# A two-layer graph network on one core: its first pass over the adjacency matrix is rebuilt

## What is computed

```python
def layer0(x, adj, w):
    A = adj + eye(4096)
    d = rsqrt(sum(A, axis=1))
    return elu(((A * d[:, None] * d[None, :]) @ x) @ w)

def layer1(x, adj, W, b):
    return relu((adj @ x) @ W.T + b)

x = layernorm(x + layer0(x, adj, w))
x = layernorm(x + layer1(x, adj, W, b))
```

## Time and profile before

| | us |
|---|---|
| median of 3 runs | 886.92 (886.02 to 890.53) |
| the profiled execution, device time | 887.87 |
| its span | 885.7 |
| TensorE busy | 793.4 (90%) |
| VectorE busy | 740.4 (84%) |
| ScalarE busy | 511.9 (58%) |
| GpSimd busy | 189.3 (21%) |
| moved by DMA | 181.71 MB, mean 205 GB/s |

### The profile page before, as it was taken

How to read it: one execution, slowest core, us unless ns; L and a number is a source line. 1 busy time by engine, 2 the same in 40 slices (tenths; PEclk the granted TensorE clock), 3 DMA queues, 4 the chain that set the end, 5 groups by cost and what they waited for, 6 DMA issues and landing times.

```text
span 885.7 us, 10783 instructions
## 1 busy us (share of the span) xinstructions
PE 793.4 (90%) x3532; PEld 653.1 (74%) x3532; DVE 740.4 (84%) x611; ACT 511.9 (58%) x1132; POOL 189.3 (21%) x181
## 2 busy tenths in 40 slices
PE   0447959599999999899999999999999999999996
PEld 0335748477878888688888888888888888888884
DVE  2368878798989998698998999898989898888963
ACT  2254646465866564368876755756653765455351
POOL 0003341341344520012221101111210322022021
PEclk9967969899999999999999999999999999999998
DMA  9999987697799999879999977989896898997500
GB/s 273 306 307 292 215 156 174 163 248 186 168 268 283 186 225 215 189 185 213 225 211 210 243 207 197 193 218 194 205 245 197 182 249 183 220 219 178 130 24 25
DMA packets 183590, 181.71 MB, mean 205 GB/s; under 512 B 6768, under 2 KB 183536, under 8 KB 183536
## 3 DMA queue, kind: packets, MB, share of 16 engines
q1 hardware_dynamic: 94704, 93.21, 45.7%
q10 hardware_dynamic: 88832, 87.83, 42.6%
HBM read 176.82 MB, written 4.19 MB: 204 GB/s over the span
## 4 chain that ended last, share of the span: by engine, by line
PE 58%; DVE 1%; issue 0%; ACT 0%; POOLq 0%; POOL 0%; DVEq 0%; ACTq 0%
PE acc L972 18%; PE acc L974 18%; PE acc L973 18%; PE proj L931 3%; PE proj L929 1%; PE acc L952 0%; DVE v_lo L684 0%; DVE stats L837 0%; DVE raw L831 0%; PE acc L1004 0%; ACT v_hi L477 0%; ACT normed L610 0%; POOLq L173 0%; DVE mean_var L842 0%; POOL rstd L445 0%
## 5 line engine op out<-in xcount | busy, mean ns | idle before, releaser
L972 PE MATMUL acc<-a_hi,v_hi 128*128 128x512 f32 x1024 | 408.4, 399 | 43.2 <-DVE a_lo L643 27.6
L457 ACT ACTIVATE a_hi<-turned 128x1024 fp32r<-128x1024 f32 x256 | 264.5, 1058 | 277.6 <-PE acc L974 131.3
L973 PE MATMUL acc<-a_lo,v_hi 128*128 128x512 f32 x1024 | 403.4, 394 | 0.0
L974 PE MATMUL acc<-a_hi,v_lo 128*128 128x512 f32 x1024 | 403.1, 394 | 0.0
L643 DVE TENSOR_TENSOR a_lo<-turned,a_hi 128x1024 fp32r<-128x1024 f32 x256 | 313.1, 1258 | 42.8 <-ACT a_hi L457 32.4
L626 DVE STREAM_TRANSPOSE turned<-raw 128x2048 f32<-128x2048 f32 x122 | 280.0, 2302 | 8.5 <-DMA raw<-in_adj_dram 2.4
L972 PEld LDWEIGHTS acc<-a_hi,v_hi 128*128 128x128 f32 x1024 | 195.4, 191 | 87.3 <-issue 30.3
L974 PEld LDWEIGHTS acc<-a_hi,v_lo 128*128 128x128 f32 x1024 | 195.1, 191 | 41.4
L973 PEld LDWEIGHTS acc<-a_lo,v_hi 128*128 128x128 f32 x1024 | 195.3, 191 | 39.9
L467 ACT ACTIVATE acc<-raw 128x256 f32<-128x256 f32 x198 | 73.0, 368 | 23.0 <-DMA raw<-in_adj_dram 21.6
L418 POOL TENSOR_TENSOR raw<-raw,x_row 128x1024 f32<-128x1024 f32 x8 | 22.6, 2830 | 179.7 <-ACT raw L513 179.7
(11 more groups left out here) (69 smaller groups left out, 413.2 us busy)
## 6 DMA issues: line engine op xcount, KB each, us to landing
raw<-in_adj_dram SPq DMA_DIRECT2D x154, 512.0 KB, 9.5
raw<-in_adj_dram ACTq DMA_DIRECT2D x154, 512.0 KB, 10.0
x_row<-in_x_dram SPq DMA_DIRECT2D x64, 128.0 KB, 6.7
out_dram<-normed ACTq DMA_DIRECT2D x28, 128.0 KB, 3.2
held<-in_adj_dram ACTq DMA_DIRECT2D x4, 512.0 KB, 12.7
held<-in_adj_dram SPq DMA_DIRECT2D x4, 512.0 KB, 12.8
partial<-in_adj_dram ACTq DMA_DIRECT2D x2, 512.0 KB, 17.0
partial<-in_adj_dram SPq DMA_DIRECT2D x2, 512.0 KB, 18.5
```

The costliest lines, as they stand in the source:

```text
L457: nc.scalar.activation(a_hi[u % 2][:, part, :], turned[u % 2][:, part, :], ACT.Copy).then_inc(s_hi, 1)
L972: pe.matmul(dst, v_hi[:, k, ch], a_hi[u % 2][:, t, :], start=begin, stop=False)
L973: pe.matmul(dst, v_hi[:, k, ch], a_lo[u % 2][:, t, :], start=False, stop=False)
L974: ins = pe.matmul(dst, v_lo[:, k, ch], a_hi[u % 2][:, t, :], start=False, stop=end)
```

## The change

**Features.** The raw x is scaled, not the projected one: `x_in` holds all of x in the memory of `v_lo`, `make_y` and `y_low` read it from SBUF, and `turn_x`, `keep_xt` and `project_x` are gone. In return `project` multiplies by w for layer 0 as it does by W.T for layer 1. w, W and b are loaded at chunk 17 and W is transposed at chunk 22. Scaled features are released tile by tile (semaphores `s_yhi`, `s_y`), four a group.

**Row sums.** The split of the 16 blocks (VectorE, ScalarE, GpSimd) is now (8, 4, 4) for chunks 0 to 7, (2, 6, 8) for the others, and (5, 5, 6) for the closing chunks of rows 2 and 3. GpSimd folds blocks of every chunk. x_row and normed together are its scratch.

**Loads.** Where a chunk's buffer was freed earlier, ScalarE issues its half ahead of the work of the current chunk (`loads_first`) and not behind it.

**The closing chain.** In rows 0 to 3 the next unit is turned between the chunk's own sums and `deg_sum`, its low half is made while GpSimd makes dinv, and `y_low` follows at once. The identity is added in one instruction instead of four.

```diff
+    loads_first = [[] for _ in chunks]
     for n in range(AHEAD, len(chunks)):
-        loads_at[max(n - AHEAD, -1 if before[n] is None else done_at[before[n]])].append(n)
...
-    DVE_BLOCKS = [10, 10, 6, 3, 3, 4, 4, 4]
-    POOL_BLOCKS, POOL_FROM = 5, 2 * PANELS
-    ACT_BLOCKS = [RB - d - (POOL_BLOCKS if row >= 2 else 0) for row, d in enumerate(DVE_BLOCKS)]
+        freed = -1 if before[n] is None else done_at[before[n]]
+        if n < FIRST_B and freed < n - AHEAD:
+            loads_first[n - AHEAD].append(n)
+        else:
+            loads_at[max(n - AHEAD, freed)].append(n)
...
+    EVEN, CLOSING, FIRST_ROWS = (2, 6, 8), (5, 5, 6), (8, 4, 4)
+    blocks_of = [FIRST_ROWS if n < 2 * PANELS else CLOSING if n < PANELS * FAST and n % PANELS == PANELS - 1 else EVEN
+                 for n in range(FIRST_B)]
+    act_degs = [sum(b[1] for b in blocks_of[:n]) for n in range(FIRST_B + 1)]
...
+    ahead_of = {n: (visits[n] or visits[n + 1])[0] for n in range(PANELS - 1, PANELS * FAST, PANELS)}
...
+    W_AT, WT_AT = PANELS * FAST + 1, PANELS * FAST + 6
...
+        x_in = nc.alloc_sbuf_tensor_at("x_in", [P, N // P, C], F32, offset=v_at + 4 * (N // P * C))
...
+        rows = sb("rows", [P, 2, GT, C])
+        x_row, normed = rows[:, 0, :, :], rows[:, 1, :, :]
...
 
-                if m >= 1 and m <= GROUPS:
-                    sp.wait_ge(s_xw, m)
+                if FAST <= m < GROUPS:
+                    sp.wait_ge(s_turn, max(units_through[n] for n in HOMES))
+                elif m == GROUPS:
+                    sp.wait_ge(s_degp, FIRST_B)
                 elif m > GROUPS:
...
+                    if m < GROUPS:
+                        home = x_in[B32 * q:B32 * (q + 1), tiles(m), :]
...
-                    n = PANELS * m + (1 if m < FAST else 2)
+                    n = PANELS * m + 2
...
-                if n == 1:
+                if n == W_AT:
+                    sp.wait_ge(s_turn, units_through[chunk_of[0, 0]])
                     sp.dma_start(w_sb[:], w.rearrange("(h c) n -> c h n", h=CH)).then_inc(s_w, 16)
```

On GpSimd and ScalarE, and the identity on VectorE:

```diff
-                i = n - POOL_FROM
+                count = blocks_of[n][2]
+                halved, folded = halved_of[count], folded_of[count][n % 2]
                 raw_loaded(pool, n)
-                mine = raw[buffer_of[n]][:, RB - POOL_BLOCKS:, :]
...
             def make_y(row):
 
                 act.wait_ge(s_dinv, row + 1)
-                act.wait_ge(s_xw, row + 1)
+                act.wait_ge(s_x, 64 * (row + 1))
...
                 for t in range(GT):
-                    ins = nc.scalar.activation(v_hi[:, tiles(row).start + 2 * t, :], proj[:, t, :], ACT.Copy,
-                                               scale=dinv[:, GT * row + t:GT * row + t + 1])
-                ins.then_inc(s_vhi, 1)
-
-            def keep_xt(row):
-
-                act.wait_ge(s_xt_mm, row + 1)
-                nc.scalar.activation(x_row[:].rearrange("p t n -> p (t n)"), proj[:].rearrange("p t n -> p (t n)"),
-                                     ACT.Copy).then_inc(s_xt, 1)
+                    k = tiles(row).start + 2 * t
+                    nc.scalar.activation(v_hi[:, k, :], x_in[:, k, :], ACT.Copy,
+                                         scale=dinv[:, GT * row + t:GT * row + t + 1]).then_inc(s_yhi, 1)
...
-                summed_first = row < FAST and at == PANELS - 1
-                if summed_first:
+                closing = row < FAST and at == PANELS - 1
+                if closing:
                     raw_loaded(act, n)
                     deg_part(n)
-                if n == PANELS - 1:
+                load_others(loads_first[n])
+                if closing:
+                    hi_and_later(ahead_of[n])
                     make_y(row)
                 for u in visits[n]:
-                    hi_and_later(u)
+                    if u not in ahead_of.values():
+                        hi_and_later(u)
                     if u == visits[n][0] and row > FAST and at == Y_AT:
                         make_y(row - 1)
                 if not visits[n] and row > FAST and at == Y_AT:
                     make_y(row - 1)
-                if not summed_first:
+                if not closing:
                     raw_loaded(act, n)
                     deg_part(n)
-                load_others(n)
-                if summed_first and n > PANELS:
-                    make_y(row)
-                if at == (2 if row < FAST else 3):
-                    keep_xt(row)
+                load_others(loads_at[n])
...
                     dve.wait_ge(s_block, row + 1)
-                    for t in range(GT):
-                        diag = turned[u % 2][:, t, :].rearrange("p (q t r) -> p t q r", q=STRIPES, r=B32)[:, t]
-                        ins = nc.vector.tensor_tensor(diag, diag, ident[:].rearrange("p (q r) -> p q r", r=B32), ALU.add)
-                    ins.then_inc(s_turn, 1)
+                    diag = diagonal_of(turned[u % 2])
+                    nc.vector.tensor_tensor(diag, diag, ident4, ALU.add).then_inc(s_turn, 1)
```

On VectorE:

```diff
             def y_low(row):
...
                 for t in range(GT):
                     k = tiles(row).start + 2 * t
-                    ins = nc.vector.scalar_tensor_tensor(out=v_lo[:, k, :], in0=proj[:, t, :],
-                                                         scalar=dinv[:, GT * row + t:GT * row + t + 1],
-                                                         in1=v_hi[:, k, :].bitcast(F32), op0=ALU.mult, op1=ALU.subtract)
-                ins.then_inc(s_v, 1)
+                    dve.wait_ge(s_yhi, GT * row + t + 1)
+                    nc.vector.scalar_tensor_tensor(out=v_lo[:, k, :], in0=x_in[:, k, :],
+                                                   scalar=dinv[:, GT * row + t:GT * row + t + 1],
+                                                   in1=v_hi[:, k, :].bitcast(F32), op0=ALU.mult,
+                                                   op1=ALU.subtract).then_inc(s_y, 1)
...
             for n in range(FIRST_B):
                 row, at = divmod(n, PANELS)
-                if n > POOL_FROM and at:
+                closing = row < FAST and at == PANELS - 1
+                if at:
                     deg_of_pool(n - 1)
-                if 0 < row <= FAST and at == 0:
-                    y_low(row - 1)
                 if row > FAST and at == 3:
                     y_low(row - 1)
-                if row < FAST and at == PANELS - 1:
+                if closing:
                     raw_loaded(dve, n)
                     deg_part(n)
+                    turn_and_low(ahead_of[n])
+                    turned_through[0] = ahead_of[n] + 1
+                    deg_of_pool(n)
                     deg_sum(row)
-                    if row < 2:
-                        deg_row(row)
-                    for u in visits[n]:
-                        turn_and_low(u)
-                        low_and_later(u)
-                    if row >= 2:
-                        deg_row(row)
-                else:
-                    for u in visits[n]:
+                    deg_row(row)
+                    low_and_later(ahead_of[n])
+                    y_low(row)
+                for u in visits[n]:
+                    if u >= turned_through[0]:
                         if units[u][3] == n:
                             raw_loaded(dve, n)
                         turn_and_low(u)
+                        turned_through[0] = u + 1
+                if not closing:
                     raw_loaded(dve, n)
                     deg_part(n)
-                    if n == 1:
-                        keep_wt()
                     if row > FAST and at == 0:
                         deg_row(row - 1)
-                    if visits[n]:
-                        low_and_later(visits[n][-1])
-                    if at == PANELS - 1:
-                        deg_sum(row)
+                if n == WT_AT + 1:
+                    keep_wt()
+                if visits[n]:
+                    low_and_later(visits[n][-1])
+                if at == PANELS - 1 and not closing:
+                    deg_of_pool(n)
+                    deg_sum(row)
```

On TensorE:

```diff
-            def turn_x(row):
-
-                pe.wait_ge(s_x, 64 * (row + 1))
...
-            def project_x(row):
-
-                pe.wait_ge(s_xt, row + 1)
...
                 if i == 0:
-                    pe.wait_ge(s_v, GROUPS)
+                    pe.wait_ge(s_wt, 1)
...
+                weights = w_sb if layer == 0 else wt_sb
                 for t in range(GT):
                     for h in range(CH):
-                        nodes = agg[:, h, P * t:P * (t + 1)]
-                        if layer == 0:
-                            ins = pe.transpose(proj[:, t, P * h:P * (h + 1)], nodes, ident[:])
-                        else:
-                            ins = pe.matmul(proj[:, t, :], nodes, wt_sb[:, h, :], start=(h == 0), stop=(h == CH - 1))
+                        ins = pe.matmul(proj[:, t, :], agg[:, h, P * t:P * (t + 1)], weights[:, h, :],
```

(49 more changed lines are left out.)

97 lines of the change are left out of this document (41 added, 56 removed).

## The result

| | before | after |
|---|---|---|
| median, us | 886.83 (4 runs) | 906.6 (4 runs, 902.65 to 913.82) |
| ratio | | 1.0224 (95% interval 1.0149 to 1.0298) |
| profiled execution, device time and span | 887.87, 885.7 | 913.82, 912.0 |

The forecast was 868, with a range of 847 to 887. The profiled execution of the changed kernel is the slowest of its four runs, 7.2 us above their median, so the times read from its trace are on the high side.

What follows compares the result with a forecast made beforehand. VectorE was taken to bound the kernel before about 225 us, TensorE after. Pass A ending at 305.5 plus 561.2 for the rest gave 866.7 us of span, 868 us forecast; 48% for 860 to 876, range 847 to 887.

Steps and rivals of the forecast that it cites:

- What bounds which part, and the cut: VectorE bounds before about 225 us, TensorE after; the sum is cut at 340.25 us, where pass A's last projection starts.
- The bill of passes B and C: From the cut to the end: layer 0 projects +20.6, dropped projection -3.6, y_low released by tile -1.2; 545.4 becomes 561.2 us.
- The point of break-even: The change breaks even if pass A ends by 324.5 us.
- Up to chunk 8: Start of pass A: chunk 7 lands at 60.2, closing work takes 9.8, VectorE starts unit 2 at 70 us, 8.9 earlier.
- The waits of the chain, -14 us: VectorE through unit 19: of 20.5 us idle in eleven waits, 6 stay.
- GpSimd, +5.7 us: VectorE through unit 19: 52 us of GpSimd folds cost it 10.4 us instead of 4.7.
- The share of a fifth: VectorE loses 20% of GpSimd's fold time through unit 19, raised from 13% measured before.
- Units 20 to 37: Late pass A: VectorE level with TensorE; 106 us instead of 115.0, so pass A ends at 305.5.
- The predicted wait of VectorE for GpSimd in a second chunk: Rows of groups 5 and 6: VectorE waits 3.5 to 4 us, twice, for the fold after dinv; +7 us.
- rival 1: Loads set pass A, which still ends at 340 us; total 903 us, chance 10%.
- Rival 2: GpSimd and VectorE exclude each other in chunks 8 to 31, a third of fold time lost: +14, 882 us, 17%.
- Rival 3: ScalarE sticks issuing loads ahead of hi and make_y, or the new chain is no shorter: 880 us, 10%.

Runs made afterwards that it cites:

- five blocks without the wait: The changed kernel with 5 of 16 blocks on GpSimd from chunk 8 on instead of 8; 885.38 us, ratio 0.9969 to the kernel before.
- The unit turned behind: Changed kernel with three GpSimd blocks and folds held until y_low is done, plus the next unit turned after deg_row; 881.52 us, against 876.38 without that turn.
- layer 0 is projected by nothing: The changed kernel with layer 0's project only transposing, the product with w left out; 888.76 us, ratio 1.0004 to the kernel before.
- short folds: The changed kernel with GpSimd's three folding adds cut to 2 columns of each block; 864.87 us, ratio 0.974 to the kernel before.
- `y_low` from PSUM: The changed kernel with x copied into PSUM by ScalarE for y_low to read, and W transposed two chunks earlier; 895.25 us, ratio 1.0088.
- three blocks in place of eight: The changed kernel with 3 blocks on GpSimd in every chunk and the next fold started only after y_low; 876.38 us, ratio 0.9861.

## Why the prediction was wrong

- **What bounds which part, and the cut.** Right. The bill of passes B and C was +15.8 and came to 560.8 - 545.4 = +15.4. The point of break-even stood at 324.5 us for the end of pass A; five blocks without the wait ended unit 37 at 325.5 in its trace, for a span of 885.3 us against 885.7 before.
- **Up to chunk 8.** Predicted 70, measured 77.75. Chunk 7 landed at 62.41 and not 60.2: 2.2 of it. `y_low` took 7.45 us and not 1.65: 5.8 of it.
- **The waits of the chain, -14 us.** Right, a little low: 6 us were to stay, and VectorE idled 4.5 in the whole window. The unit turned behind shows one of its parts.
- **GpSimd, +5.7 us. This is the step that failed.** The sum held 10.4 us of loss, a fifth of 52 us of folds, for units 2 to 19 alone. Measured there were 26.6, 16.2 more: 15.7 in low halves and 10.9 in `y_low`. Two things had been left out. First, of `y_low` I wrote that it "reads two operands in SBUF like the low halves, and joins in this", and then priced it at 1.65 us. It lost 24.4 us in the whole of pass A. It was the worst placed instruction of all: GpSimd makes dinv, starts a fold of 1024 columns at once, and `y_low` needs dinv. At the closings of rows 1 to 3 the two always meet (7.45, 7.36 and 6.87 us), so a share drawn from chance meetings did not apply. Second, the folds of units 20 to 37 cost nothing in the sum. There low halves lost 13.5 us and `y_low` 6.6. With the 5.8 us before unit 2 this is 5.8 + 16.2 + 20.1 = 42 of the 45.7 us by which pass A ended late.
- **The share of a fifth.** It was not far off for low halves, 29.1 of 148.2 us, a fifth, though a share from folds of five blocks (9% over all of the old pass A) was no ground for it. VectorE's idle time does not explain the difference: with five blocks on the changed kernel it idled 7.0 us in units 2 to 19, against 22.6 in the kernel before, and low halves lost 9% in both. All these are figures of the slowest execution; where layer 0 is projected by nothing, low halves lost 7.4 us less in the same pass A.
- **Units 20 to 37.** Predicted 106, measured 128.2. From `fold_degrees` of row 4 to that of row 7 the changed kernel took 127.9 us, the short folds 107.8. The predicted wait of VectorE for GpSimd in a second chunk was there (3.76 us at 230.27, against 1.08 in the next row); `y_low` and low halves made up 20.1 of the 22 us. TensorE was busy 106.6 us there, against 102.2 with short folds, where its clock was 0.98 and not 0.93; how much of this was on the path was not separated.
- **The rivals.** The time landed next to rival 1's 903 us, but by another mechanism: its waits for chunks are not there, and short folds alone, with the same loads, moved the mark from 345.21 to 296.18. Rival 2 was the mechanism. Its 882 raised the loss from a fifth to a third of 106 us of folds, but the sum that it was added to held only the 10.4 us of units 2 to 19, and `y_low` was in neither. I gave slower 13%. Rival 3 was not seen: from chunk 7 to unit 37 VectorE waited 3.0 us for `a_hi` in all.

The rest of the sum was nearly right: without its 10.4 us for the folds it gives 858, and short folds took 864.87. That 868 lies within 4 us of that run is luck: it has 10 us of folds in it that cost nothing there.

## What to carry to other kernels

Before work is moved to GpSimd, list VectorE's instructions with two operands in SBUF that can run beside it, in every stage, and put a price on each in the sum. A meeting can cost nearly the whole GpSimd instruction: a `y_low` instruction of 0.47 us took up to 2.6 beside adds of 2.4. A share measured with short folds is too low for long ones: low halves lost 9% of the fold time with five blocks on GpSimd and 15 to 20% with eight. Where the order itself makes the two meet (GpSimd produces a value, starts something long, and VectorE needs the value), put a wait on GpSimd or take one operand from PSUM. The waits, together with three blocks in place of eight, turned a kernel 2.2% slower into one 1.4% faster.

## What the hardware showed that I had not expected

- A string of short instructions is hurt most. Four of 0.47 us became 7.36 us, since after each of them GpSimd's next instruction got its turn; the four took 2.57, 1.49, 0.94 and 2.59 us.
- Instructions with one operand in SBUF kept their time beside folds of the same size: transposes 2.30 us, adds of partial sums 1.21, `y_low` from PSUM 1.65 for four.
- The loss is not in proportion to the fold: eight blocks cost VectorE 54.0 us, five 17.9, for 148 and 110 us of folds.
